# A slot order for a six-layer attention and feed-forward pipeline: turnings at the head of TensorE's slot, copies ahead of exponentials, half of the rotation's additions on VectorE

## What is computed

```python
for i in range(DEPTH):                     # 6
    x = attn_layer(shift_tokens(x), Wqkv[i], q_scale[i], k_scale[i], Wo[i]) + x
    x = ffn_layer(shift_tokens(x), ln_g[i], ln_b[i], W1[i], b1[i], W2[i], b2[i]) + x
```

## Time and profile before

| | |
|---|---|
| three executions | 3173.82, 3157.74, 3172.20; median 3172.2 |
| the profiled execution | 3166.98, its span 3165.2 |
| TensorE (PE) matmul busy | 2656.3, 84% of the span |
| VectorE (DVE) | 1647.5, 52% |
| ScalarE (ACT) | 1206.0, 38% |
| GpSimd (POOL) | 1128.7, 36% |
| mean granted TensorE clock | 0.899 of full speed |

### The profile page before, as it was taken

The page is one execution under the profiler, slowest core; times in us unless marked ns, Lnnn a source line. Parts: engine busy times, 40 slices in busy tenths (PEclk is TensorE's granted clock), DMA queues, the critical chain, the costliest instruction groups (busy, mean ns, idle before and its releaser), DMA issues. The chain is left out here.

```text
span 3165.2 us, 46116 instructions
## 1 busy us (share of the span) xinstructions
PE 2656.3 (84%) x15697; PEld 1564.9 (49%) x15697; DVE 1647.5 (52%) x3712; ACT 1206.0 (38%) x3124; POOL 1128.7 (36%) x956
## 2 busy tenths in 40 slices
PE   5979999658976888888888888888878798699798
PEld 2436776314543555555555555555534544455343
DVE  4445555436635666666666666666445322263333
ACT  1423222003512565556565556565423011145121
POOL 2000000010114978787778787777310000100000
PEclk8989999659957999999999999999978598699799
DMA  2100000000001000000000000000000000000010
GB/s 63 31 1 0 0 0 0 0 7 9 2 1 44 1 21 8 12 18 14 12 11 14 22 8 9 21 8 8 1 14 2 14 27 14 13 9 2 30 31 25
DMA packets 42398, 41.63 MB, mean 13 GB/s; under 512 B 6924, under 2 KB 31283, under 8 KB 42179
## 3 DMA queue, kind: packets, MB, share of 16 engines
q1 hardware_dynamic: 42178, 38.82, 4.7%
HBM read 33.23 MB, written 0.52 MB: 11 GB/s over the span
## 5 line engine op out<-in xcount | busy, mean ns | idle before, releaser
L2980 PE MATMUL ps<-l1fb_wqkv,l1fb_xs 128*128 128x512 f32 x576 | 304.1, 638 | 115.4 <-ACT l1fb_kT L2922 40.0
L2788 POOL TENSOR_TENSOR l1fb_p<-l1fb_p,l1fb_rden 128x640 f32<-128x640 f32 x192 | 240.8, 1254 | 254.3 <-DVE l1fb_rden L2851 254.3
L2846 DVE TENSOR_REDUCE l1fb_shift<-ps 128x4 f32<-128x640 f32 x192 | 158.2, 824 | 326.4 <-PE ps L3010 326.3
L2780 POOL TENSOR_TENSOR l1fb_rinv<-l1fb_ssq,neghalf 128x8 f32<-128x8 f32 x192 | 316.8, 1650 | 0.2
L2936 ACT ACTIVATE l1fb_p<-ps,l1fb_shift 128x128 f32<-128x128 f32 (+1 forms) x768 | 281.2, 385 | 2.0 <-DVE l1fb_shift L2846 1.7
L2778 POOL TENSOR_TENSOR l1fb_qk<-l1fb_qk,l1fb_r 128x512 f32<-128x512 f32 x192 | 243.7, 1269 | 5.0 <-DVE l1fb_r L2837 5.0
L2782 POOL TENSOR_TENSOR l1fb_qk<-l1fb_qk,l1fb_rinv 128x512 f32<-128x512 f32 x192 | 200.7, 1046 | 15.1
L2980 PEld LDWEIGHTS ps<-l1fb_wqkv,l1fb_xs 128*128 128x128 f32 x576 | 96.6, 191 | 207.9 <-issue 57.4
L2943 ACT ACTIVATE l1fb_pT<-ps 128x512 f32<-128x512 f32 x192 | 114.6, 597 | 194.1 <-PE ps L3032 194.1
L2917 ACT ACTIVATE l1fb_sq<-ps 128x512 f32<-128x512 f32 x192 | 114.7, 597 | 186.2 <-PE ps L2980 160.0
L2936 ACT ACTIVATION_READ_ACCUMULATOR l1fb_p<-ps,l1fb_shift 128x1 f32 x768 | 162.7, 212 | 0.0
(11 more groups left out here) (719 smaller groups left out, 5837.0 us busy)
## 6 DMA issues: line engine op xcount, KB each, us to landing
l1fb_wqkv<-in_L_ffn_Wqkv SPq DMA_DIRECT2D x24, 256.0 KB, 2.7
l3f_w<-in_L_ffn_W SPq DMA_DIRECT2D x21, 256.0 KB, 3.0
l2f_w<-in_L_ffn_W SPq DMA_DIRECT2D x16, 256.0 KB, 3.0
l1fb_wqkv<-in_L_ffn_Wqkv SPq DMA_DIRECT2D x6, 512.0 KB, 4.5
l1fb_wo<-in_L_ffn_Wo SPq DMA_DIRECT2D x6, 512.0 KB, 4.0
l1fb_w<-in_L_ffn_W SPq DMA_DIRECT2D x6, 341.0 KB, 2.9
l3x_k<-l3x_k SPq DMA_DIRECT2D x8, 128.0 KB
l1fb_w<-in_L_ffn_W SPq DMA_DIRECT2D x6, 128.0 KB
```

What stands on the lines that cost most here:

```text
L2780: nc.gpsimd.tensor_tensor(w.rinv[:, u, :], w.ssq[:, u, :], chip.neghalf[:, 0:8], ALU.pow).then_inc(*w.unit_norm.end(f"rinv{u}"))
L2788: nc.gpsimd.tensor_tensor(p, p, w.rden[:, c, :, :].rearrange("p j q -> p (j q)").unsqueeze(2).to_broadcast([P, 2 * QT, SEEN]), ALU.mult)\
L2846: nc.vector.tensor_reduce(w.shift[:, c, :, :], ps[:, bank:bank + 2, 0:2 * SEEN].rearrange("p j (q n) -> p j q n", n=SEEN), AX.X, ALU.max, ...
L2980: nc.tensor.matmul(ps[:, PROJ_BANK(u), :], w.xs[:, x.odd, q * P:(q + 1) * P], w.wqkv[:, col:col + 512], start=True, stop=True)\
```

## The change

In each of TensorE's slots both transposing groups now come first, that of the next unit's queries and keys (t) and that of the weights (T), and then the scores S; before it was S, T, then feed-forward work, then t. In slot 1 the first projection moves behind S. On ScalarE the two copies e and c come ahead of the exponentials X; before, c stood ahead of X and e behind it; q of slot 0 moves into slot 1. The plans of VectorE and GpSimd keep their order. Apart from that, the addition `qk += r2` of the even groups moves from GpSimd's n to VectorE's r, where it stands between the sum of squares and the clamp.

```diff
-PE_PLAN = """S0 T6' gate01' t4' V6' gate2' p0    S1 T7' value01' t5' V7' value2' p1    S2 T0 y2' t6' V0 p2    S3 T1 y1 t7' V1 p3
-             S4 T2 mean t0 V2 p8 p4              S5 T3 var t1 V3 p9 p5                 S6 T4 t2 V4 p10 p6      S7 T5 spread t3 V5 p11 p7""".split()
+PE_PLAN = """t4' T6' S0 gate01' V6' gate2'    t5' T7' S1 p0 value01' V7' value2' p1    t6' T0 S2 y2' V0 p2    t7' T1 S3 y1 V1 p3
+             t0 T2 S4 mean V2 p8 p4           t1 T3 S5 var V3 p9 p5                    t2 T4 S6 V4 p10 p6     t3 T5 S7 spread V5 p11 p7""".split()
 DVE_PLAN = """inv7' att5' max0 edge6' r7' tab    inv0 att6' max1 edge7' g0' g1' r0 g2'  inv1 att7' max2 edge0 x2' r1  inv2 att0 max3 edge1 r2 x1
               inv3 att1 max4 edge2 centre r3     inv4 att2 max5 edge3 vareps r4          inv5 att3 max6 edge4 diag xs r5  inv6 att4 max7 edge5 xn r6""".split()
-ACT_PLAN = """c6' X0 e4' gelu0' gelu1' gelu2' q0    c7' X1 e5' q1    c0 X2 e6' q2    c1 X3 e7' q3
-              c2 X4 e0 v8 q4    c3 X5 e1 v9 q5    c4 X6 e2 v10 q6    c5 X7 e3 v11 q7""".split()
+ACT_PLAN = """e4' c6' X0 gelu0' gelu1' gelu2'    e5' c7' q0 X1 q1    e6' c0 X2 q2    e7' c1 X3 q3
+              e0 c2 X4 v8 q4    e1 c3 X5 v9 q5    e2 c4 X6 v10 q6    e3 c5 X7 v11 q7""".split()
...
     def unit_norm(x, u):
-        after(eng, w.rot, f"rot{u}", x)
-        nc.gpsimd.tensor_tensor(w.qk[:, u, :], w.qk[:, u, :], w.r2[:, u % 2, :], ALU.add).then_inc(*w.unit_norm.end(f"add{u}"))
+        if u % 2:
+            after(eng, w.rot, f"rot{u}", x)
+            nc.gpsimd.tensor_tensor(w.qk[:, u, :], w.qk[:, u, :], w.r2[:, 1, :], ALU.add).then_inc(*w.unit_norm.end(f"add{u}"))
         after(eng, w.rot, f"clamp{u}", x)
...
-        after(eng, w.unit_norm, f"add{(u - 2) % QK}", x.past(0 if u >= 2 else 1))
+        if u % 2:
+            after(eng, w.unit_norm, f"add{(u - 2) % QK}", x.past(0 if u >= 2 else 1))
...
         nc.vector.tensor_reduce(w.ssq[:, u, :], heads(w.sq[:, u % 2, :]), AX.X, ALU.add).then_inc(*w.rot.end(f"ssq{u}"))
+        if u % 2 == 0:
+            after(eng, w.rot, f"rot{u}", x)
+            nc.vector.tensor_tensor(r1, r1, r2, ALU.add).then_inc(*w.rot.end(f"add{u}"))
         after(eng, w.rot, f"ssq{u}", x)
```

More of the change, by code:

```diff
@@ L2692, in l1_ffn_layers @@
         w.xsteps = Steps(sem("xsteps"), ["xs"])
-        w.rot = Steps(sem("rot"), [f"{s}{u}" for u in range(QK) for s in ("rot", "ssq", "clamp")])
+        w.rot = Steps(sem("rot"), [f"{s}{u}" for u in range(QK) for s in (("rot", "ssq", "clamp") if u % 2 else ("rot", "ssq", "add", "clamp"))])
         w.max, w.inv = Steps(sem("max"), each("max", ITEMS)), Steps(sem("inv"), each("inv", ITEMS))
@@ L2698, in l1_ffn_layers @@
         w.X, w.kept, w.gelu = Steps(sem("X"), each("X", ITEMS)), Steps(sem("kept"), each("c", ITEMS)), Steps(sem("gelu"), each("gelu", 3))
-        w.unit_norm = Steps(sem("unit_norm"), [f"{s}{u}" for u in range(QK) for s in ("add", "rinv", "qk")])
+        w.unit_norm = Steps(sem("unit_norm"), [f"{s}{u}" for u in range(QK) for s in (("add", "rinv", "qk") if u % 2 else ("rinv", "qk"))])
         w.scaled, w.root = Steps(sem("scaled"), each("s", ITEMS)), Steps(sem("root"), ["root"])
```

## The result

| | before | changed |
|---|---|---|
| median | 3173.0 us (3157.7 to 3182.6) | 3317.8 us (3311.3 to 3329.0) |
| profiled execution, its span | 3167.0, 3165.2 | 3315.0, 3313.2 |
| mean granted clock of TensorE | 0.899 | 0.893 |

The ratio is 1.0465, with a 95% interval of 1.0413 to 1.0516: the changed kernel is slower by 4.65%. The forecast was 3287 in a range of 3235 to 3345.

A forecast was written before the change was run, and what follows sets the result against it. Waits for ScalarE's copies bound today's slots; the new order closes a ring through att. Units go from 52.04 to 56.8: 4.8 in 23 units is 110, plus 10 for the clock, on 3167: 3287 us, range 3235 to 3345.

The forecast's parts named there:

- Both turnings ahead of the scores: t, T before scores: slots 4-7 last scores' start to att's end plus 1.09: 6.72, 5.99, 6.88, 6.71 us.
- The ring: Loop over TensorE and VectorE, once a slot: att, t, T, scores, maxima, edge, extra work, rotation, reciprocal, next att.
- The addition on VectorE: Slots 1, 3, 5, 7: addition moved from GpSimd into the ring, 0.5 us each (0.4 to 0.7).
- Slot 2: 6.73 us, today 5.32: scores to att's end 6.14, less 0.5 for a freed wait, plus 1.09.
- Slot 3: 7.6 us: scores to att's end 7.05, less 0.5, plus 1.09; addition lies beside the 16 y1 matmuls.
- Slots 0 and 1: Together 15.2 us, today 14.6: 7.63 with T waiting for the third gelu, plus 7.5, plus 0.06.
- Copies ahead of exponentials: ScalarE: both TensorE waits go, but the edge transpose holds the values, 6.23 us a slot; no gain counted.
- the clock's term: TensorE's clock halving after stops at slot heads: 1.5 us more in every third unit, about 10 us (0 to 35).
- rival four: TensorE's clock falls in every unit: +35 us instead of +10, 3312 us, inside the range; 12%.
- the units at the ends: 23 of 24 units each cost 4.8 us more; the last, with no next unit to project, costs nothing.
- rival two: VectorE's addition waits for a wide GpSimd operation, about 1 us, four times a unit: +92, 3379 us; 4%.
- Rivals one and three: One: att in time, -22 us, 3145, 6%. Three: ring and freed waits cancel within 0.5% (16 us), 4%.

The follow-up runs named there:

- the sixth experiment: Kernel before with only ScalarE's second copy put ahead of the exponentials in slots 4 to 7, TensorE's order untouched: 3096.8 us, 0.9772.
- the first experiment: Changed kernel with TensorE's old order put back, ScalarE's new order and the addition on VectorE kept: 3292.3 us, 1.0377.

## Why the prediction was right, and where it wasn't

**Both turnings ahead of the scores: right.** The ring holds seven of the eight slots, the wait of t for att is now TensorE's largest (154.6 us), and cutting it at att, with the same work, takes 2.5 us from slots 4 to 7. The rule "scores to the end of att, plus 1.09" gave 6.72, 6.49, 6.88 and 7.21 for these; the undisturbed unit has 6.69, 6.43, 7.09 and 7.14. The unit came out at 56.6 for 56.8. The 1.09 is partly luck: t and T take 0.90 and not 1.03, and the event 0.15 and not 0.06. The wait for att, forecast as 0.5 and more in nearly every slot, is that in five of eight; it is 0.41 and 0.16 at the heads of slots 5 and 6, and at the head of slot 4 there is none.

**The addition on VectorE: right,** 0.49 in the trace for 0.5, between 0.35 and 0.47 a slot when it is taken back, and nothing outside the ring.

**Slot 2: right** (6.65 for 6.7). **Slot 3: the number was right by luck** (7.51 for 7.6). The ring doesn't hold this slot. At its end t starts at 1271.00 straight after the projection, without a wait, and att had ended at 1270.81. TensorE's own work with the 16 matmuls of y1 fills the slot, as it did before (7.48); it stays at 7.5 with the addition taken back and with the ring cut. **Slots 0 and 1: right** (15.07 for 15.2), with the wait of T for the gelu and a wait of 2.04 for att at slot 2's head.

**Copies ahead of exponentials: right in what was argued,** that the edge transpose takes the place of the waits removed. I drew too little from it: the sentence "the gain is eaten" holds for the new TensorE order. In the old one the same copies are worth 74 us (3096.8 against 3170.8), as the sixth experiment shows. The forecast didn't need that, but it is where the gain lay.

**Sum: the clock's term failed.** I took about 10 us, from one stop in every third unit. The layer stage went from 11 to 28 stretches, and the 21 units show 31 us, with the loop's turn in it, which the forecast doesn't have; keeping TensorE busy at the heads of slots 1 and 2 alone gave 24 of it back in the median. That is nearly rival four, which I had given 12%. The mechanism and its places were as said, the stops at the heads; the failing step is "1.5 us in every third unit more". Measured it is 17 more stretches in 23 units, three in four, and at most 31 / 17 = 1.8 us each: the price was near, the frequency was not. I had no row that says how often a stop of that length brings the clock down, and chose near the low end of 0 to 35, where the two stops of a unit (T's and att's) against the one of before spoke for the upper half. After such a stop:

```profile
1674.93 0.63 PE L3001 MATMUL ps<-ident,l1fb_qk 128*128 128x128 f32 x4 [2.05 <-DVE l1fb_attT L2865]
...
1676.19 1.17 PE L3015 MATMUL ps<-l1fb_kT,l1fb_qT 64*128 64x128 f32 x8
1677.30 2.07 PE L3109 MATMUL ps<-l1fb_g,l1fb_w 128*128 128x256 f32 x4
```

The scores take 1.17 and not 0.77, and the first four y2 matmuls 2.07 (all six take 1.56 at full clock): slot 2 is 8.25 in such units, not 6.65.

**Sum: the units at the ends.** The first two cost 14.7 for 9.6 and the last, which I took as free, 4: it has no t, but T still stands ahead of the scores. Together 9 us. I had priced every unit by the steady one. In all the span grew by 148 for 120: the clock with the loop's turn 21 more, the ends 9, work outside these units 3, and the undisturbed units 5 less.

**The range.** Its high end doesn't follow from its own terms: on top of 3287, 25 more for the clock, 14 for the addition at 0.7 in three slots of 23 units and 46 for half of rival two give 3372, not 3345. The result lies below both.

**Rival two: a real mechanism at another instruction.** The addition was held up by GpSimd's wide multiplication once in 96 times (1.01; the median is 0.68), because in this kernel's ring it comes when GpSimd has run dry, as said. But VectorE's product for the diagonals, which I had taken as untouched, does meet it. Its durations before (minimum, median, maximum in ns):

```profile
L2884 DVE TENSOR_TENSOR l1fb_dsq<-ident,l1fb_rstd x24: 424/426/426, 1100.4 to 2282.3; 128x256 f32<-128x256 f32 x24
```

and after:

```profile
L2889 DVE TENSOR_TENSOR l1fb_dsq<-ident,l1fb_rstd x24: 425/664/668, 1113.9 to 2428.4; 128x256 f32<-128x256 f32 x24
```

That is the 0.2 by which slot 6 is longer than forecast. And in the first experiment, where the addition isn't behind GpSimd's work but beside it, it took 1.1 in the median: rival two's price, about 0.4 each more than its 0.68 and not 1.

**Rivals one and three:** att is never in time in slots 4 to 7, and nothing cancelled.

Not tried: whether a second bank for the turned queries would open the ring in the changed order. It would need the accumulation memory laid out anew.

## What to carry to other kernels

Before an instruction goes to the head of an in-order queue, list everything that it waits for, the last reader of its output buffer included: that reader's place in *its* queue becomes part of the loop, and a slot lasts as long as the longest way round. If a copy comes too late, move the copy in its own queue first, with one word in one list, and leave the queue that waits for it alone. Orders on two engines are only good as a pair: half of a change can be worse than all of it or than none.
